# Expert weights split during the projections, one residual row per token, the norm applied per expert tile, part of the lists scattered later

## The reference

```python
x = x + attn(layernorm(x), Wq_down, Wk_down, Wv_down, Wq_up_c, Wq_up_e, Wk_up_c, Wk_up_e, Wv_up, Wc)
xf = layernorm(x)                                  # x is (4, 2048, 256): 8192 tokens
logits = xf @ Wr + br                              # 8 experts
topk_w, topk_idx = top_k(logits, 2);  topk_w = softmax(topk_w)
h = relu(einsum('th,ehf->etf', xf, W1) + b1)       # F = 512
y = einsum('etf,efh->eth', h, W2) + b2
x = x + sum over the two chosen experts of topk_w * y
```

## Time and profile before

| what | us |
|---|---|
| median of 3 runs | 2852.18 (2844.67 to 2854.98) |
| profiled execution, time | 2858.26 |
| its span | 2856.5 |
| PE busy | 2441.9 (85%) |
| DVE busy | 2109.3 (74%) |
| ACT busy | 1469.4 (51%) |
| POOL busy | 768.3 (27%) |
| mean granted clock of PE | 0.907 of 2.4 GHz |

### The profile page before, as it was taken

The page is one execution under the profiler, slowest core; times in us unless marked ns, Lnnn a source line. Parts: engine busy times, 40 slices in busy tenths (PEclk is TensorE's granted clock), DMA queues, the critical chain, the costliest instruction groups (busy, mean ns, idle before and its releaser), DMA issues. The chain is left out here.

```text
span 2856.5 us, 49091 instructions
## 1 busy us (share of the span) xinstructions
PE 2441.9 (85%) x15842; PEld 1377.5 (48%) x15842; DVE 2109.3 (74%) x5168; ACT 1469.4 (51%) x2478; POOL 768.3 (27%) x1056
## 2 busy tenths in 40 slices
PE   6785389999998989989999999998777359999998
PEld 6674133333333333333333333332445248988987
DVE  3886589888888888878889888850466537766666
ACT  2442047677776766767777777776432112222222
POOL 1444011111011011011111101111177635555554
PEclk8887579899999999989999999997788679999999
DMA  3665922243144044134134404000687133333332
GB/s 138 235 238 179 127 33 28 37 60 45 22 61 59 10 58 60 17 49 59 21 45 60 49 17 62 7 8 4 200 205 178 51 106 112 110 103 92 110 104 80
DMA packets 170133, 231.21 MB, mean 81 GB/s; under 512 B 71716, under 2 KB 127398, under 8 KB 163249
## 3 DMA queue, kind: packets, MB, share of 16 engines
q1 hardware_dynamic: 145920, 169.45, 29.3%
q0 software_dynamic: 22640, 56.39, 6.6%
q10 hardware_dynamic: 1344, 2.45, 0.2%
HBM read 140.12 MB, written 89.93 MB: 81 GB/s over the span
## 5 line engine op out<-in xcount | busy, mean ns | idle before, releaser
L763 ACT ACTIVATE prob<-ps_s 128x512 f32<-128x512 f32 (+5 forms) x1620 | 1079.0, 714 | 539.7 <-PE ps_s L857 537.0
L784 DVE TENSOR_REDUCE maxes<-ps_m 128x2 f32<-128x1024 f32 x768 | 914.0, 1221 | 116.4 <-PE ps_m L892 113.3
L892 PE MATMUL ps_m<-k_st,q_st 48*128 48x512 f32 (+3 forms) x2560 | 612.3, 449 | 116.2 <-DMA v_sb<-v_dram 56.4
L857 PE MATMUL ps_s<-q_st,k_st 50*128 50x512 f32 (+3 forms) x2560 | 617.1, 417 | 75.6 <-ACT prob L763 55.7
L875 PE MATMUL ps_o<-prob,v_sb 128*17 128x512 f32 (+3 forms) x5120 | 627.0, 563 | 4.1 <-issue 2.9
L741 POOL TENSOR_SCALAR_AFFINE_SELECT prob<-prob 128x256 f32<-128x256 f32 x512 | 204.0, 408 | 1499.6 <-ACT prob L763 1370.2
L892 PEld LDWEIGHTS ps_m<-k_st,q_st 48*128 48x128 f32 x2560 | 278.3, 194 | 579.5 <-DVE maxes L784 260.8
L788 DVE CUSTOM_DVE_ANT_0 junk<-ps_m,causal 128x128 f32<-128x128 f32 (+3 forms) x1024 | 453.3, 485 | 81.4 <-PE ps_m L892 80.0
L857 PEld LDWEIGHTS ps_s<-q_st,k_st 50*128 50x128 f32 x2560 | 322.8, 193 | 308.8 <-ACT prob L763 234.1
L1650 ACT ACTIVATE h_hi<-ps_turned 128x512 fp32r<-128x512 f32 x142 | 85.1, 600 | 253.0 <-PE ps_turned L1749 131.4
L87 PE MATMUL ps_out<-experts_hi,h_lo 128*128 x568 | 172.7, 304 | 0.1
(11 more groups left out here) (182 smaller groups left out, 3096.6 us busy)
## 6 DMA issues: line engine op xcount, KB each, us to landing
parts_dram<-parts SPq DMA_DIRECT2D x64, 512.0 KB, 3.4
q_st<-parts_dram SPq DMA_DIRECT2D x96, 256.0 KB, 15.5
k_st<-parts_dram SPq DMA_DIRECT2D x96, 256.0 KB, 17.3
v_dram<-v_out SPq DMA_DIRECT2D x16, 544.0 KB, 5.3
v_sb<-v_dram SPq DMA_DIRECT2D x16, 544.0 KB, 25.3
xin<-in_L_attn_x SPq DMA_DIRECT2D x16, 512.0 KB, 5.6
y_dram<-y_sb SPq DMA_DIRECT2D x64, 128.0 KB, 2.0
y_in<-y_dram SPq DMA_DIRECT2D x16, 512.0 KB
```

What stands on the lines that cost most here:

```text
L763: last_exp = nc.scalar.activation(prob[:, at:at + n, lo:TB], bank[:, 0:n, lo:TB], ACT.Exp, scale=DH ** -0.5)
L784: return nc.vector.tensor_reduce(maxes[:, 2 * pair:2 * pair + 2, qt, kc], bank[:, :, :], AX.X, ALU.max)
L857: mm = nc.tensor.matmul(ps_s[k % 2][:, i, lo:TB], k_st[half(h % 2, ROWS), w % BUFS, h // 2, kt * P:(kt + 1) * P], q_st[half(h % 2, ROWS), ...
L892: mm = nc.tensor.matmul(ps_m[slot][:, i, 0:wide], q_st[half(i, STACK), w % BUFS, pair, qt * P:(qt + 1) * P], k_st[half(i, STACK), w % BUFS ...
```

## The change

- `project` also takes W1 and W2. Each of its 16 rounds loads one chunk of each (ffn_raw), copies the high part on ACT and subtracts the low part on POOL, 128x1024 elements each, and stores both to `split_dram`. `mix` loads these pieces into SBUF, 1 MB per block, and splits nothing any more.
- In `mix` a token's row in `rows_dram` is x1 alone, 1 KB. Tokens are laid out as p*4+j, so that rows of x, y and rows_dram are 4 KB pieces. The normalisation xn that the router needs is done by ACT; an entry of the lists holds token, gate, scale and shift. PE's order in a step is mix_heads, turn xn, count, turn_y, route, turn_logits. From block 9 on (LATE) `mix` scatters only the first choice's entries; the 28 missing scatters are issued by POOL in pass one of `experts`.
- In `experts` ACT applies scale and shift to the gathered rows. Pass one writes x1 and the sum to `pairs_dram` (2 KB per token), which pass two gathers. There are 8 row buffers and 12 lists; the result is written into the row buffer itself. In pass two DVE adds the rows of tile s-2 in round s (LAG). The biases are loaded by ACT, and DVE waits for them after its first low_rows.

```diff
@@ project
+            def load_ffn(n, u):
+                sp.dma_start(ffn_raw[:, u, 0, :], w1_v[n, :, :]).then_inc(ffn_in[u], 16)
+                sp.dma_start(ffn_raw[:, u, 1, :].rearrange("p (o c) -> p o c", c=C), w2_v[n, :, :, :]
+                             ).then_inc(ffn_in[u], 16)
+            def store_ffn(n, u):
+                sp.wait_ge(ffn_lo_made, n + 1)
+                sp.sem_inc(sp_alone, 1)
+                for to, part in zip(split_v, (ffn_hi, ffn_lo)):
+                    sp.dma_start(to[:, :, bass.ds(n, 1), :].rearrange("p l n f -> p (l n) f"),
+                                 part[:, u, :, :].bitcast(F32)).then_inc(ffn_out[u], 16)
...
                     store(2 * k + u, u)
+                    store_ffn(2 * k + u, u)
+                    load_ffn(2 * k + 2 + u, u)
...
+                        pool.wait_ge(ffn_hi_made, n + 1)
+                        nc.gpsimd.tensor_tensor(out=ffn_lo[:, u, :, :], in0=ffn_raw[:, u, :, :],
+                                                in1=ffn_hi[:, u, :, :].bitcast(F32),
...
+                act.wait_ge(ffn_in[u], 32 * k + 32)
+                act.wait_ge(ffn_out[u], 32 * k + 16 * PRIMED)
+                nc.scalar.copy(ffn_hi[:, u, :, :], ffn_raw[:, u, :, :]).then_inc(ffn_hi_made, 1)
@@ mix
-                for j in range(n * TILES, (n + 1) * TILES):
-                    for i in range(TOP):
+                for i in range(TOP if n < LATE else 1):
+                    for j in range(n * TILES, (n + 1) * TILES):
                         pool.indirect_dma_start(
                             list_dram[:, :], bass.IndirectOffsetOnAxis(ap=slots[:, j, i:i + 1], axis=0),
...
+            def normalise(n):
+                act.wait_ge(scale_made, n + 1)
+                for j in range(TILES):
+                    last = nc.scalar.activation(xn[:, n % 2, j, :], x1[:, n % 2, j, :], ACT.Identity,
+                                                scale=rstd[:, n % 2, j:j + 1], bias=shift[:, n % 2, j:j + 1])
@@ experts
-LISTS = 8
-ROWBUFS = 6
-ZBUFS = 4
-EARLY_ROWS = ROWBUFS - 1
+LISTS = 12
+ROWBUFS = 8
+XBUFS = 2
+YBUFS = 4
+LAG = 2
+EARLY_ROWS = ROWBUFS - 2
+LATE_LISTS = [s for s in range(4, PASS_TILES) if s % 3][:NT - LATE * TILES]
...
+            def free(s):
+                if s >= ROWBUFS:
+                    pool.wait_ge(scattered[s % ROWBUFS], 16 * (s // ROWBUFS))
             def gather(s):
                 pool.wait_ge(list_in[s % LISTS], 16 * (s // LISTS + 1))
-                if s >= ROWBUFS:
-                    pool.wait_ge(z_made, s - ROWBUFS + 1)
+                free(s)
...
             for s in range(TILE_COUNT):
+                scatter(s)
                 ahead = s + ROWBUFS - 1
                 if ahead < PASS_TILES or PASS_TILES + EARLY_ROWS <= ahead < TILE_COUNT:
                     gather(ahead)
                 elif ahead < TILE_COUNT:
                     gather_first_half(ahead)
-                scatter(s)
+                if s in LATE_LISTS:
+                    scatter_entries(LATE * TILES + LATE_LISTS.index(s))
...
+            def normalise(s):
+                act.wait_ge(list_in[s % LISTS], 16 * (s // LISTS + 1))
+                act.wait_ge(gathered[s % ROWBUFS], 16 * (s // ROWBUFS + 1))
+                if s >= XBUFS:
+                    act.wait_ge(x_turned, s - XBUFS + 1)
+                nc.scalar.activation(xn[:, s % XBUFS, :], rows[:, s % ROWBUFS, 0:C], ACT.Identity,
+                                     scale=lists[:, s % LISTS, 2:3].bitcast(F32),
+                                     bias=lists[:, s % LISTS, 3:4].bitcast(F32)).then_inc(xn_made, 1)
...
             for s in range(TILE_COUNT):
+                if s + 4 < TILE_COUNT:
+                    normalise(s + 4)
                 if s + 3 < TILE_COUNT:
                     high_rows(s + 3)
                 if s + 2 < TILE_COUNT:
...
-                add_rows(s, es[s % 2])
+                add_second_bias(s, es[s % 2])
+                if s < PASS_TILES:
+                    add_rows(s)
+                elif s >= PASS_TILES + LAG:
+                    add_rows(s - LAG)
                 if s + 2 < TILE_COUNT:
                     low_hidden(s + 2)
+            for s in range(TILE_COUNT - LAG, TILE_COUNT):
+                add_rows(s)
...
             def turn_rows(s):
-                pe.wait_ge(gathered[s % ROWBUFS], 16 * (s // ROWBUFS + 1))
+                pe.wait_ge(xn_made, s + 1)
```

More of the change, by code:

```diff
@@ L27 @@
 PARTS = 2
+WCH = 512
+TOP = 2
+CHUNKS = 2 * E * F * C // (P * WCH)
+HALF = CHUNKS // 2
 PRIMED = 1
@@ L187, in project @@
         v_stored = [sem(f"v_stored{u}") for u in range(2)]
+        ffn_in = [sem(f"ffn_in{u}") for u in range(2)]
+        ffn_hi_made = sem("ffn_hi_made")
+        ffn_lo_made = sem("ffn_lo_made")
+        ffn_out = [sem(f"ffn_out{u}") for u in range(2)]
+        sp_alone = sem("sp_alone1")
+        act_alone = sem("act_alone1")
+        w1_v = w1.rearrange("e (a p) f -> (e a) p f", p=P)
+        w2_v = w2.rearrange("e (a o p) c -> (e a) p o c", p=P, o=WCH // C)
+        split_v = [part.rearrange("p (l n) f -> p l n f", l=2) for part in split_dram]
         x_v = x.rearrange("b (c j p) d -> (b c) p j d", p=P, j=TILES)
@@ L918, with mix @@
 NT = B * T // P
-RAWS = 4
-XB = 3
-def mix(nc, x, y_dram, wc, wr, br, w1, w2, tile_numbers, w_sb, row_of, expert_of, rows_dram, list_dram):
-    w_hi, w_lo = w_sb
+WLOADS = 4
+LATE = 9
+YB = 3
+XB = 2
+def mix(nc, x, y_dram, wc, wr, br, split_dram, tile_numbers, w_sb, row_of, expert_of, entry, slots, rows_dram,
+        pairs_dram, list_dram):
     with ExitStack() as ctx:
@@ L1107, in scatter @@
                             entry[:, j, i, :], None).then_inc(scattered, 16)
-            for c in range(RAWS):
-                split(c)
-            pool.wait_ge(prefilled, 3 * 16)
+            pool.wait_ge(prefilled, 4 * 16)
             for n in range(NB + 2):
@@ L1114, in _ @@
                     scatter(n - 2)
-                for c in range(RAWS + 2 * n, min(RAWS + 2 * n + 2, CHUNKS)):
-                    split(c)
-            pool.wait_ge(scattered, 16 * TOP * NT)
+            pool.wait_ge(scattered, 16 * (NT + LATE * TILES))
         @block.scalar
@@ L1165, in _ @@
                     copy_turned(yt)
-                for c in range(RAWS + 2 * n, min(RAWS + 2 * n + 2, CHUNKS)):
-                    split(c)
-            act.wait_ge(prefilled, 3 * 16)
+                if 1 <= n <= NB:
+                    act.wait_ge(routed, n)
+                    if n > 1:
+                        act.wait_ge(logits_turned, n - 1)
+                    nc.scalar.activation(by_expert[:, :], ps_r[0:E, :], ACT.Identity,
+                                         bias=br_sb[:, 0:1]).then_inc(by_expert_made, 1)
+            act.wait_ge(prefilled, 4 * 16)
         @block.vector
@@ L1341, in _ @@
                     after_norm()
-                    if n >= 2:
-                        dve.wait_ge(xn_stored[n % 2], 16 * (n // 2))
-                        dve.wait_ge(rows_turned, units(n - 2, True) + 2)
-                    for j in range(TILES):
-                        last = ts(xn[:, n % 2, j, :], x_in[:, u, j, :], mv[:, j, 0:1], rstd[:, j:j + 1],
-                                  ALU.subtract, ALU.mult)
-                    last.then_inc(xn_made, 1)
+                    stt(out=shift[:, n % 2, :], in0=mv[:, :, 0], scalar=-1.0, in1=rstd[:, n % 2, :],
+                        op0=ALU.mult, op1=ALU.mult).then_inc(scale_made, 1)
+                if normal:
+                    dve.wait_ge(scale_made, n + 1)
+                    here = slice(n * TILES, (n + 1) * TILES)
+                    for word, values in ((2, rstd), (3, shift)):
+                        nc.vector.tensor_copy(entry[:, here, :, word].bitcast(F32),
+                                              values[:, n % 2, :].unsqueeze(2).broadcast_to([P, TILES, TOP]))
                 if m >= 0:
@@ L1554, in experts @@
         late_index = sem("late_index")
-        scattered = [sem(f"scattered{u}") for u in range(ZBUFS)]
+        scattered = [sem(f"scattered{u}") for u in range(ROWBUFS)]
+        listed = sem("listed")
+        xn_made = sem("xn_made5")
         x_turned = sem("x_turned")
@@ L1650, in high_hidden @@
                 nc.scalar.activation(h_hi[:, s % 2, :], ps_t[s % 2][:, :], ACT.Relu).then_inc(h_hi_made, 1)
+            for bias, to, width in ((b1, b1_sb, F), (b2, b2_sb, C)):
+                act.dma_start(to[:, :, :].rearrange("p e n -> p (e n)"),
+                              bias.rearrange("(a e) n -> a (e n)", a=1).broadcast_to([P, E * width])
+                              ).then_inc(biases_in, 16)
+            normalise(0)
+            normalise(1)
             high_rows(0)
+            normalise(2)
             high_rows(1)
+            normalise(3)
             high_hidden(0)
```

281 lines of the change are left out of this document (136 added, 145 removed).

## The result

The changed kernel takes 3115.97 us (median of 4 runs, 3102.94 to 3126.08), the kernel before, run beside it, 2852.75 (2844.67 to 2854.98): a ratio of 1.0926, 95% interval 1.0875 to 1.0977. The forecast was 3100 in a range of 2990 to 3175. The profiled execution took 3109.82 us, span 3108.1, so the spans differ by 251.6 us.

A forecast was written before the change was run, and what follows sets the result against it. The experts were taken as PE-bound and mix's round as set by POOL, with a one-round ring of waits deciding pass two after the change. Terms summed to +247.5 on 2858.26 us, 3106 profiled, 3100 as median; range 2990 to 3175.

The forecast's parts named there:

- The ring: Pass two: waits from gather through normalise, y, z and scatter to next gather span one round, 7.94 us a tile; +275 us.
- Pass boundary: Between the experts' passes: with the lag, z(71) is wanted two tiles later; -10 us.
- Tail: End of the kernel: three z and three scatters after the last y instead of one; +4 us.
- The clock: Pass two: PE, idle over half of a round, is granted near 0.5 of its clock; nothing added.
- Late lists: Pass one of experts: 28 list scatters on POOL, mostly taken by slack; +10 us, bounds below 0 and above 84.
- Mix: Mix, blocks 9 to 15: four scatters instead of eight, round 9.6 us instead of 13.7; -26 us, bounds -8 and -35.
- Attention: Attention stage: nothing edited, its time stays; 0.
- Projections: Projections: added loads and stores fill the queues, round at least 13.7 us; +16 us, bounds 0 and +45.
- slots to list: Last slots to first list load: POOL done sooner, DVE's tables last, 15.4 us instead of 25.3; -10 us.
- list to first `h`: First list load to first `h`: biases issued by ACT at once, 14.0 us instead of 25.55; -11.5 us, bounds -5 and -17.
- The rival of the other side: Pass two: look-ahead suffices, the 275 falls away, the rest is -27.5, 2825 us; chance 10%.

The follow-up runs named there:

- Experiment 4: Changed kernel with all list scatters back in the mix stage (no late lists), lag 2 kept; 3100.67 us, ratio 1.0835.
- experiment 7: Changed kernel with lag 0, all lists in mix and one extra gather of 1 KB rows by POOL in 28 pass-one tiles; 2894.09 us (one run).
- 6: Changed kernel with lag 0, all lists in mix and an extra 128x512 POOL subtraction in 28 pass-one tiles; 2844.64 us (one run).
- experiment 2: Changed kernel with a lag of 1 instead of 2 in pass two; 2878.04 us, ratio 1.009.
- Experiment 1: Changed kernel with lag 0 instead of 2 in pass two; 2865.75 us, ratio 1.0016.
- experiment 8: Changed kernel with lag 0 and the 28 late list scatters in every second tile of pass one instead of two of three; 2874.41 us, ratio 1.0099.

## Why the forecast was right, and where it was off

**The ring: right, a little too long.** Forecast 7.94 us a tile, measured 7.64 in one turn and 7.72 over 64 tiles. Every piece is there in the order forecast. Scatter to gather (1.33) and gather to normalise (3.45 against 3.40) hit; the normalisation, which had no row, was 0.51 against 0.45. Too large were low_rows (0.34 against 0.46) and y to z (0.33 against 0.57): a step from one instruction to the next on one engine costs less than when it has to wait for something. Four kernels show the structure, each by another edit (last 64 tiles, 7.19 us each in the changed kernel): lag 0 gives 3.54 us, lag 1 gives 3.83, a ninth buffer with lag 2 gives 3.73, ACT's order alone 4.63. In the steady stretch alone the changed kernel has 7.72, and lag 1 and the ninth buffer 3.99 and 3.93, 0.1 us over its half. The ring is as long as what it is made of, and the pace is that length over the number of rounds that it may span. The 64 tiles cost 64 x (7.72 - 3.64) = 261 us, not 275.

The gather can be set beside the rule again. The Trainium skill's page "DMA: Bandwidth & Descriptors", section "Anatomy of one DMA — SWDGE (gpsimd) path", leads to an estimate of 2.6 us for it; the row of pass two has 3.45 from the issue's start to the first use, as the earlier trace rows had 3.40, both for 2 KB rows. The measurement decides. For 1 KB rows the first gather of pass one after has 2.94 (2254.66 to 2257.60).

**Pass boundary: right.** 252.6 less 261 leaves -8 for it and the last tiles, against -10. Before, the eight tiles lose 10.6 us there (38.8 - 28.2); after, z of tile 71 comes 14.0 us behind that of tile 70, which with the lag is three rounds, 10.6 us at PE's pace, so 3.4 are lost. **Tail:** +1.9 against +4.

**The clock: wrong.** I expected PE near half its clock where it idles for more than half of a round. It was granted 0.82, where a stretch of mix had 0.59 with 22.72 of 50 us busy (third row). The step took that one stretch for a rule; nothing in the sum hung on it.

**Late lists: the step that failed.** Forecast +10, measured +54. I argued that the row gathers and scatters, issued all through the experts, hold nothing, and so took a value near nothing out of 0 to 84. The trace of before showed the mechanism but I read it as one of mix. On the chips that show it, it is one of POOL's issuing: with two issues in 3.53 us POOL pauses for 0.9 us in each tile and the signals get through; a third issue closes the pause, five DMAs stand in a row, PE's signal from the end of the run comes 1.0 to 1.4 us after the last, and the next z, and so the next run, starts from there. What on the chip holds the signal, no trace shows. Experiment 4 puts the whole 54 us on the list scatters; 7 shows that a gather does the same; 6 that POOL's computing costs less than half of it, with runs of four issues and late signals in that too.

**Mix: mechanism right, size too small.** With four scatters a block the signals come in time: in the timeline after, `place` starts 0.1 us behind PE's count in three blocks (2188.32, 2197.10, 2205.88), and the rounds there are 8.6 to 8.8 us, the next 7.7, where I took 9.6. So -35 instead of -26, at the bound given.

**Attention: a miss of 19 us within what equal code differs by.** No line of it is edited, and I put 0. Over all profiled executions with the same attention code it lasts from 1608.0 us (experiment 2) to 1665.0 (experiment 4), and with it goes the granted clock. The windows of 395 to 2000 us, first in experiment 2 and then in experiment 4:
```profile
395.00:2000.00 1605.00, 1483.79 (x10388) 609.18 (x10391) 1330.74 (x2899) 1161.50 (x1853) 202.74 (x511) 0.97 0.27 38
```
```profile
395.00:2000.00 1605.00, 1491.51 (x10152) 612.47 (x10156) 1330.16 (x2896) 1125.10 (x1799) 200.16 (x503) 0.94 0.27 37
```
At 0.97 in the same 1605 us 1853 ACT instructions get done, at 0.94 1799. Both are of one chip. What moves the clock between executions is open. Two single profiles can differ by up to 57 us from this alone (1665.0 - 1608.0); the runs' medians and the other stages carry less.

**Projections (+12.7 for +16), slots to list (-8.4 for -10), list to first `h` (-8.1 for -11.5): right.** The round there is 14.0 to 14.1 us, with the transfers at 93% and 325 GB/s, as good as full. Between list and `h` the first x_lo starts at 2259.76, and `h` 3.9 us later.

**By the sum:** the four terms that were off (ring -14, attention -19, mix -9, late lists +44) nearly cancel: that they do is luck. The total, 16 us above the forecast, looks better than its parts; 12 of the 16 are only that before's profiled execution was 6 us above its median and the changed kernel's 6 below.

The rival of the other side, that the look-ahead suffices, failed on what it needed itself: a ring that spans three rounds. Experiment 1 is that kernel, and it takes 2866 us, against 2825 forecast for it, the late lists being most of the difference.

## What to carry to other kernels

Before lagging, reordering or buffering in a software pipeline, write down the loop that runs from "buffer is free" through transfer and engines back to "buffer is free", add up its length, and count how many rounds it may span; the pace is the larger of the busiest engine and length over rounds. A lag of two rounds took two of three rounds from the look-ahead and cost 250 us; the lag back restored all of it, one more buffer nearly all. And an engine that issues transfers has a limit besides its own time: look for the pause that other engines' signals go through before moving issues into a stage that "has room".

## What the runs showed that I had not expected

- On two chips PE's signals to ACT and DVE are late when POOL has issued four or more indirect DMAs back to back, at 1.27 to 1.31 us each: those from late in a run arrive 1.0 to 1.7 us after the run's last issue, up to 4.4 us late in the rows above. Gathers of 1 KB rows and scatters of 16-byte entries do so alike.
- The first issues of a run hold nothing, or nearly nothing. In experiment 1, from 2325 to 2500 us, ACT and DVE waited for PE 69 times while a run had got no further than its third issue, and none of these waits lasted over 0.5 us past PE's end; from the fifth issue on 14 of 29 lasted over 0.8 us. No count of issues is a rule, though: in experiment 7, 7 of 95 waits lasted over 0.8 us within the first three.
- The same code on a third chip shows no hold: `place` follows PE by 0.11 us in the middle of a run. The kernel before, the only one that ran on all three, is faster there by 28 to 35 us. Why chips differ is open.
- With three issues in a row forced into each second tile two tiles take 9.2 us instead of 7.1 (intervals of 6.7 and 2.5 us in experiment 8), though POOL's five issues fill only 6.5 us.
- PE was granted 0.82 of its clock in a stretch where it was busy for 62% of the time in short bursts.
